# Back-to-back making of a head's two bf16 maxima parts on VectorE, in an attention and expert kernel on one Trainium2 core

## The chip, the cores and the metric

The kernel runs on one core of one Trainium2 chip. The metric is the device time of one execution in microseconds; the median of three runs of the kernel before is 1437.19 us (1435.57 to 1438.66). Engines are named as in the profile: PE is TensorE, PEld its weight loads, DVE is VectorE, ACT is ScalarE, POOL is GpSimd and SP is the engine that issues the DMAs.

## What is computed

A layer with gated attention and a gated mixture of experts. The attention, cut to what matters here:

```python
att = jnp.einsum('bhqd,bhkd->bhqk', q, k) * scale          # 4 batches, 16 heads, 512 queries, 512 keys, D=16
att = jnp.where(causal[None, None], att, -jnp.inf)
y = jnp.einsum('bhqk,bhkd->bhqd', jax.nn.softmax(att, axis=-1), v)
attc = jnp.einsum('bhqd,bhkd->bhqk', qc, kc) * scale       # the same queries on 1601 context rows
y = y + jnp.einsum('bhqk,bhkd->bhqd', jax.nn.softmax(attc, axis=-1), vc)
...
x = x + jnp.tanh(g_xattn[0]) * (y @ Wp + bp)
x = x + jnp.tanh(g_ffn[0]) * ffn(layernorm(x))             # a shared expert and 2 of 7 routed ones
```

Both softmaxes subtract a row's maximum, so each of the 64 (batch, head) pairs, called heads below, needs the maxima of its 512 queries over its own and over the cross scores before its exponentials are made.

## The kernel before

The program is written by hand: every engine has its own instruction stream and waits on counting semaphores, and there is no scheduler. It has three stages: preparation (projections, split into three bf16 parts, to about 153 us), the 64 heads (to about 936 us), and the projection, router and experts.

**One head.** A head's scores are computed twice on PE. The first time is for the maxima: 16 pieces (`MAX_PIECES`: 12 blocks of 128 queries by 512 context rows, one tail, three of the causal scores), each a product into a PSUM bank (`max_product`, mostly L525) and a reduction of it on DVE (`reduce_bank`, L1214). The second time the scores are made with keys on the partitions (`score`, L625 and L628), in 8 groups (`GROUPS`); two more rows of the stacked operands, made of the negated maxima, subtract each query's maximum in the product itself. ACT takes the exponential of each group (L967), and PE multiplies it with the values in 4 phases (`values`, L643).

**The maxima's way to the scores.** `max_parts(v, i)` on DVE makes them for head v in three instructions:

- i=0, L1226: the maximum over the five columns of `mx`, into `mneg[:, 1, :]`; signals `m_all`
- i=1, L1229: the negated maxima rounded to bf16, the high part, into `mparts[:, 0]`; waits for `m_all`, signals `m_hi`
- i=2, L1232: the rest, the low part, into `mparts[:, 1]`; waits for `m_hi`, signals `m_split`

Then `max_rows` on PE (L565 and L566) waits for `m_split` and turns them into rows by a product with the identity, ACT copies these to `rowst` (`rows`, L927), SP sends them to the stacked operand (`rows_load`, L448), and the next head's first score waits for the landing (`rows_ready`).

**The order on PE** is `schedule()`: in the step of head u it goes through groups g = 0 to 7; each brings the maxima's products 2g and 2g+1 around its scores. Product c of the step belongs to head u+1 (its pieces 8 to 15) for c below `HALF` = 8, and to head u+2 (its pieces 0 to 7) from c = 8 on. So the last piece of head u+1 is c = 7. The transposing product ("rows") comes after c = 11 and in front of the second value block (`values` 1). After product 7 come value block 0, the product that normalizes the head before ("norm", L692), and product 8.

**The banks.** Products c, "norm" and "rows" take three PSUM banks in turn (`ENTRIES`, `RING` = 3). `bank_free` therefore makes "rows" wait until DVE has reduced product 9, by the semaphore `max_red`, and only then does `max_rows` wait for `m_split`. Product 11 waits for the reduction of product 8 in the same way.

**The loop.** `run_steps` writes out heads 0 and 1, then a loop of 15 turns with four heads in its body, then heads 62 and 63. Inside the loop the values waited for lie in registers, so the engines' streams hold register additions.

Of the kernel before, what the change touches and what calls it, by code (L numbers as in the profile page):

```python
# [91 lines left out]
HALF = NMAX // 2  # L92
# [58 lines left out]
def program(nc, a):  # L151
    ctx = ExitStack()
    with ctx:
# [1020 lines left out]
        def _(dve):  # L1174
# [41 lines left out]
            def reduce_piece(u, c):  # L1216
                dve.wait_ge(S["max_mm"], u * NMAX + (c + 1))
                v, piece = (u + 1, c + HALF) if c < HALF else (u + 2, c - HALF)
                reduce_bank(v, piece, bank_of("max", c)).then_inc(S["max_red"], 1)

            def max_parts(v, i):

                if i == 0:
                    if not (isinstance(v, int) and v == 0):
                        dve.wait_ge(S["max_red"], v * NMAX + (NMAX - MAXED))
                    dve.tensor_reduce(mneg[:, 1, :], mx[:, :, :], AX_X, ALU.max).then_inc(S["m_all"], 1)  # L1226
                if i == 1:
                    dve.wait_ge(S["m_all"], v + 1)
                    dve.tensor_scalar(mparts[:, 0, :, :], mneg[:, :, :], -1.0, None, ALU.mult).then_inc(S["m_hi"], 1)  # L1229
                if i == 2:  # L1230
                    dve.wait_ge(S["m_hi"], v + 1)
                    dve.scalar_tensor_tensor(out=mparts[:, 1, :, :], in0=mneg[:, :, :], scalar=-1.0,  # L1232
                                             in1=mparts[:, 0, :, :], op0=ALU.mult, op1=ALU.subtract
                                             ).then_inc(S["m_split"], 1)
# [4 lines left out]
            for n, p in enumerate(pieces):  # L1239
# [24 lines left out]
                if p[0] == "max":  # L1264
                    _, v, c = p
# [25 lines left out]
            def reciprocals(u):  # L1291

                dve.wait_ge(S["sums_in"], u)
                if not (isinstance(u, int) and u == 1):
                    dve.wait_ge(S["y_parts"], u - 1)
                dve.reciprocal(rsum[:, :, :], sums[:, :, 2:4, D]).then_inc(S["rsum_ready"], 1)

            def step(u, r, prev, nxt, nxt2):
                for c in range(NMAX):
                    if (c < HALF and nxt) or (c >= HALF and nxt2):  # L1300
                        reduce_piece(u, c)
                    if nxt and HALF - 1 <= c < HALF + 2:
                        max_parts(u + 1, c - HALF + 1)
                    if prev and c == RSUM_AT:
                        reciprocals(u)

            run_steps(dve, step)
            reciprocals(NU)

# [276 lines left out]
```

## Time and profile before

| | us |
|---|---|
| median of 3 runs | 1437.19 |
| the profiled execution, its own time | 1437.22 |
| its span in the trace | 1435.5 |
| PE busy in the span | 1378.3 (96%) |
| DVE busy | 868.1 (60%) |
| ACT busy | 727.9 (51%) |
| POOL busy | 365.7 (25%) |

The busy time of PE holds modelled ends, and consecutive matmuls overlap in the records: two products of 512 columns stand some 0.22 us apart and are 0.38 us long each. So a short stop of PE shows less by its idle time than by the distance between starts. The same holds for DVE, where a reduction of 0.69 us is followed by the next instruction's start after 0.61 us.

### The profile page before, as it was taken

The page shows a single profiled execution, that of the slowest core. Times are in us where ns is not written, and L with a number is a line of the kernel's source. Part 1 is how long each engine was busy: PE and PEld are TensorE (multiplying, and loading weights), DVE is VectorE, ACT ScalarE, POOL GpSimd, SP SyncE. Part 2 cuts the span into 40 slices and gives each one's busy share as a digit, 9 for nine tenths or more (in the row PEclk, how much of TensorE's full clock was granted, in tenths as well). Part 3 has the DMA queues.
Part 4 walks back from the last instruction along what each step waited for, and adds up shares of the span by engine and source line. Part 5 has one row for each costly group of instructions (what it writes and reads, how often), then busy time and mean ns, then how long its engine had stood idle before and what let it go on. Part 6 is the DMA issues. An engine that isn't in the chain of part 4 may idle for free.

```text
span 1435.5 us, 27237 instructions
## 1 busy us (share of the span) xinstructions
PE 1378.3 (96%) x7688; PEld 697.9 (49%) x7689; DVE 868.1 (60%) x1804; ACT 727.9 (51%) x1107; POOL 365.7 (25%) x743
## 2 busy tenths in 40 slices
PE   7889899999999999999999999989999999999997
PEld 4445333333333333333333333354556677777775
DVE  6658688888888888888888888734532222222221
ACT  4534567767666767667676767652100222222221
POOL 5455322222222222222222222210000223323232
PEclk9989999999999999999999999999999999999999
DMA  7654211111111111111111111039003111212211
GB/s 240 206 159 146 85 52 51 49 49 48 48 46 49 50 51 50 49 49 47 47 48 48 50 51 50 18 143 364 0 1 117 40 30 29 37 29 31 34 29 23
DMA packets 57711, 98.43 MB, mean 69 GB/s; under 512 B 7441, under 2 KB 42001, under 8 KB 56657
## 3 DMA queue, kind: packets, MB, share of 16 engines
q1 hardware_dynamic: 50384, 88.10, 18.5%
q0 software_dynamic: 7296, 9.97, 4.3%
q8 instruction: 15, 0.25, 0.1%
q14 instruction: 16, 0.12, 0.0%
HBM read 69.20 MB, written 28.58 MB: 68 GB/s over the span
## 4 chain that ended last, share of the span: by engine, by line
PE 80%; issue 5%; DVE 4%; ACT 1%; DVEq 0%; DMA 0%; POOL 0%; POOLq 0%; SPq 0%; ACTq 0%
PE ps L643 18%; PE ps L808 13%; PE ps L625 10%; PE ps L525 10%; PE ps L821 7%; PE ps L760 5%; PE ps L771 3%; PE ps L692 3%; PE ps L539 2%; PE ps L832 2%; PE ps L628 2%; DVE mx L1214 1%; PE ps L529 1%; PE ps L566 1%; PE ps L599 1%
## 5 line engine op out<-in xcount | busy, mean ns | idle before, releaser
L1214 DVE TENSOR_REDUCE mx<-ps 128x1 f32<-128x512 f32 (+1 forms) x832 | 521.3, 663 | 127.0 <-PE ps L525 96.7
L967 ACT ACTIVATE arena<-ps 128x1024 f32<-128x1024 f32 (+1 forms) x512 | 484.5, 995 | 152.4 <-PE ps L625 148.7
L643 PE MATMUL ps<-arena 128*32 128x512 f32 (+5 forms) x2432 | 290.1, 524 | 0.6 <-ACT arena L967 0.4
L625 PE MATMUL ps<-arena 98*128 98x512 bf16 x832 | 264.2, 380 | 4.5 <-DMA arena<-rowst 4.5
L525 PE MATMUL ps<-arena 96*128 96x512 bf16 x768 | 263.4, 382 | 4.3 <-DVE arena L1279 2.4
L808 PE MATMUL ps<-arena,work 128*128 x608 | 186.4, 460 | 0.6 <-issue 0.6
L1116 POOL TENSOR_SCALAR_AFFINE_SELECT arena<-arena 128x128 f32<-128x128 f32 x256 | 74.8, 292 | 437.4 <-ACT arena L967 427.5
L525 PEld LDWEIGHTS ps<-arena 96*128 96x128 bf16 x768 | 74.3, 97 | 174.0 <-DVE mx L1214 103.2
L1489 DVE TENSOR_TENSOR work<-work,ps 128x352 f32<-128x352 f32 x76 | 39.6, 521 | 179.1 <-ACT work L1033 179.1
L808 PEld LDWEIGHTS ps<-arena,work 128*128 128x128 f32 x608 | 112.6, 190 | 57.4 <-issue 1.1
L1214 DVE TENSOR_REDUCE mneg<-ps 128x2 f32<-128x512 f32 (+2 forms) x192 | 112.4, 640 | 23.0 <-PE ps L535 23.0
L1033 ACT ACTIVATE work<-ps 128x352 f32<-128x352 f32 x76 | 35.2, 463 | 164.6 <-PE ps L808 164.6
L1158 POOL DMA_INDIRECT out<-bv,slot_table x38 | 59.8, 1575 | 207.3 <-DVE bv L1495 197.5
L643 PEld LDWEIGHTS ps<-arena 128*32 128x32 f32 (+1 forms) x2432 | 56.7, 108 | 113.5 <-issue 110.2
L625 PEld LDWEIGHTS ps<-arena 98*128 98x128 bf16 x832 | 76.7, 98 | 65.5 <-DMA arena<-rowst 5.7
L821 PE MATMUL ps<-arena,work 128*128 (+1 forms) x456 | 105.0, 379 | 0.8 <-ACT work L1039 0.8
L821 PEld LDWEIGHTS ps<-arena,work 128*128 128x128 f32 (+1 forms) x456 | 83.7, 190 | 11.4 <-issue 1.1
L1148 POOL DMA_INDIRECT wp<-xn_rows,slot_table x38 | 37.7, 992 | 173.4 <-DVE slot_table L1478 137.6
L1038 ACT ACTIVATE work<-ps 128x256 f32<-128x256 f32 x76 | 29.1, 382 | 99.7 <-PE ps L832 99.6
L760 PE MATMUL ps<-xnT,arena 128*128 128x512 f32 x176 | 77.1, 594 | 0.4 <-DVE work L1321 0.4
L1076 POOL TENSOR_TENSOR work<-arena,work 128x400 bf16<-128x400 f32 (+2 forms) x56 | 58.1, 1037 | 68.2 <-ACT work L919 67.4
L911 ACT ACTIVATE work<-ps,bqk 128x400 bf16<-128x400 f32 (+2 forms) x56 | 35.4, 632 | 64.7 <-DMA k_parts<-work 37.4
(157 smaller groups left out, 1411.0 us busy)
## 6 DMA issues: line engine op xcount, KB each, us to landing
arena<-in_experts SPq DMA_DIRECT2D x8, 2176.0 KB, 11.8
arena<-k_parts SPq DMA_DIRECT2D x64, 198.1 KB
arena<-k_parts SPq DMA_DIRECT2D x64, 132.1 KB
k_parts<-work SPq DMA_DIRECT2D x24, 300.0 KB, 4.2
q_parts<-work SPq DMA_DIRECT2D x16, 384.0 KB, 3.5
arena<-q_parts SPq DMA_DIRECT2D x64, 96.0 KB
arena<-k_parts SPq DMA_DIRECT2D x64, 66.0 KB
arena<-q_parts SPq DMA_DIRECT2D x64, 64.0 KB
```

Source lines behind the costliest of these rows:

```text
L525: mm = pe.matmul(out, qx[:, qt * P:(qt + 1) * P], ks[0:KROWS, T + j * CHUNK:T + (j + 1) * CHUNK], start=True, stop=True)
L625: mm = pe.matmul(bk[:, 0:w], kst[r][0:KROWS + MROWS, T + kt * P:T + (kt + 1) * P], qst[r][0:KROWS + MROWS, 1, :], start=True, stop=True)
L643: mm = pe.matmul(ps[32 * q:32 * q + VW, 6, b0:b1], vst[0:kn, r % VR, TT + kt if cross else kt, :], pr[0:kn, c0:c0 + b1 - b0], start=(phase ...
L692: mm = pe.transpose(out[:, t * P:(t + 1) * P], osb[:, t * P:(t + 1) * P], ident[:, :])
L760: mm = pe.matmul(ps[:, 2 * (k0 % 2) + j, :], wgus[:, k, w0:w0 + P], xnT[:, k, tb * T:(tb + 1) * T], start=(k == 0), stop=(k == 1))
L808: mm = pe.matmul(ps[:, 2 * c + j, 0:CH], xgT[:, b, k, :], weights[:, bass.ds(e, 1), o:o + CH], start=(k == 0), stop=(k == 1))
L821: mm = pe.matmul(ps[:, 4, 0:C], hidT[0:m, it, :], weights[0:m, bass.ds(e, 1), o:o + C], start=(it == 0), stop=(it == IT - 1))
L967: act.activation(pr[:, c0:c0 + n], ps[:, 2 * (g % 2):2 * (g % 2) + 2, :].rearrange("p b n -> p (b n)")[:, 0:n], ACT.Exp, scale=SCALE).then ...
L1076: pool.tensor_tensor(cut[:, s % NB, place_of(t)[2], 0:w], res[:, s % NB, 0:w], cut[:, s % NB, place_of(t)[1], 0:w], ALU.subtract).then_inc ...
L1116: pool.affine_select(out=exps, in_=exps, pattern=[[1, P]], compare_op=ALU.is_ge, fill=0.0, base=0, channel_multiplier=-1).then_inc(S["mask ...
L1158: pool.indirect_dma_start(out=a["out"], out_offset=bass.IndirectOffsetOnAxis(slot_table[:, i, 1:2], 0), in_=yt[:, i % 2, :], in_offset=Non ...
L1214: return dve.tensor_reduce(m, out, AX_X, ALU.max)
```

## The change

In the step of head u, DVE made the three instructions of `max_parts(u + 1, ...)` with a reduction between each two of them: reduction 7, part 0, reduction 8, part 1, reduction 9, part 2, reduction 10. They now stand behind reduction 7 together, in front of reduction 8. PE's order does not change, nor do those of ACT, POOL and SP.

```diff
                 for c in range(NMAX):
                     if (c < HALF and nxt) or (c >= HALF and nxt2):
                         reduce_piece(u, c)
-                    if nxt and HALF - 1 <= c < HALF + 2:
-                        max_parts(u + 1, c - HALF + 1)
+                    if nxt and c == HALF - 1:
+                        for i in range(3):
+                            max_parts(u + 1, i)
                     if prev and c == RSUM_AT:
                         reciprocals(u)
```

VectorE in a head of the loop, before. `mneg<-ps` are the reductions of products 6 and 7 (causal pieces), `mx<-ps` those of products 8, 9 and on; REGISTER_ALU and ISA are instructions of the engine's sequencer that compute a semaphore's value, and two of them carry a wait.

```order
L1214 TENSOR_REDUCE mneg<-ps 128x1 [waits max_mm]
L1225 ISA
L1226 TENSOR_REDUCE mneg<-mx 128x4 [waits max_red]
L1217 REGISTER_ALU
L1203 REGISTER_ALU [waits max_mm]
L1214 TENSOR_REDUCE mx<-ps 128x1 [waits m_all]
L1229 TENSOR_SCALAR mparts<-mneg 128x8 [waits m_all]
L1217 REGISTER_ALU
L1214 TENSOR_REDUCE mx<-ps 128x1 [waits max_mm]
L1232 SCALAR_TENSOR_TENSOR mparts<-mneg,mparts 128x8 [waits m_hi]
L1217 REGISTER_ALU
L1214 TENSOR_REDUCE mx<-ps7 128x1 [waits max_mm]
```

The same place of the same head in the changed kernel:

```order
L1214 TENSOR_REDUCE mneg<-ps 128x1 [waits max_mm]
L1225 ISA
L1226 TENSOR_REDUCE mneg<-mx 128x4 [waits max_red]
L1228 REGISTER_ALU
L1229 TENSOR_SCALAR mparts<-mneg 128x8 [waits m_all]
L1232 SCALAR_TENSOR_TENSOR mparts<-mneg,mparts 128x8 [waits m_hi]
L1217 REGISTER_ALU
L1214 TENSOR_REDUCE mx<-ps 128x1 [waits m_all,max_mm]
L1217 REGISTER_ALU
L1214 TENSOR_REDUCE mx<-ps 128x1 [waits max_mm]
L1217 REGISTER_ALU
L1214 TENSOR_REDUCE mx<-ps7 128x1 [waits max_mm]
```

Both parts moved ahead of the reductions of products 8 and 9, and the register instruction of L1203, which waited for product 8, is gone: the reduction carries both waits itself.

TensorE around the transposing product (L566), which is the same in both kernels; L625 and L628 are scores, L525 the maxima's products 9, 10 and 11:

```order
L525 MATMUL ps<-arena 128x512 [waits max_red]
L525 MATMUL ps7<-arena 128x512 [waits norm_evac]
L656 REGISTER_ALU
L625 MATMUL ps<-arena 128x512 [waits exp_done]
L628 MATMUL ps<-arena 128x256
L628 MATMUL ps<-arena 128x128
L551 REGISTER_ALU
L525 MATMUL ps<-arena 128x512 [waits max_red]
L551 REGISTER_ALU
L566 MATMUL ps<-identb,mparts 16x128 [waits m_split,max_red]
L636 REGISTER_ALU [waits exp_done]
L643 MATMUL ps<-arena 32x512 [waits masked]
```

Nothing moves here: L566 keeps its two waits, for the bank (`max_red`) and for the parts (`m_split`).

## Rows read from the trace of the kernel before

**Rows 1.** The page's first line.
```profile
span 1435.5 us, 27237 instructions
```
**Rows 2.** Busy time by stretch, the heads: us, engines, granted clock, DMA.
```profile
162.00:936.00 774.00, 763.18 (x5229) 292.50 (x5226) 624.69 (x1240) 542.19 (x687) 182.80 (x560) 1.00 0.15 47
```
**Rows 3.** Line 566, the transposing product: durations; what ended idle time before.
```profile
L566 PE MATMUL ps<-identb,mparts x64: 216/218/223, 132.4 to 932.6; 128*16 128x128 bf16 x64
...
  DVE mparts L1232: 29.2, 86
```
**Rows 4.** Timeline of DVE, a head of the loop: start us, us, instruction.
```profile
707.40 0.17 DVE L1226 TENSOR_REDUCE mneg<-mx 128x4 f32<-128x16 f32 x1
708.38 0.69 DVE L1214 TENSOR_REDUCE mx<-ps 128x1 f32<-128x512 f32 x1 [0.81 <-PE ps L525]
708.99 0.16 DVE L1229 TENSOR_SCALAR mparts<-mneg 128x8 bf16<-128x8 f32 x1
709.06 0.68 DVE L1214 TENSOR_REDUCE mx<-ps 128x1 f32<-128x512 f32 x1
709.66 0.16 DVE L1232 SCALAR_TENSOR_TENSOR mparts<-mneg,mparts 128x8 bf16<-128x8 f32 x1
```
**Rows 5.** Timeline of PE, the same head: products 8, 9 with 10, 11, transpose.
```profile
707.87 0.38 PE L525 MATMUL ps<-arena 96*128 96x512 bf16 x1
...
708.53 0.59 PE L525 MATMUL ps<-arena 96*128 96x512 bf16 x2
...
709.34 0.38 PE L525 MATMUL ps<-arena 96*128 96x512 bf16 x1
709.87 0.22 PE L566 MATMUL ps<-identb,mparts 128*16 128x128 bf16 x1
```
**Rows 6.** The fourth head of the loop's body: DVE, then PE.
```profile
734.49 0.16 DVE L1232 SCALAR_TENSOR_TENSOR mparts<-mneg,mparts 128x8 bf16<-128x8 f32 x1
```
```profile
733.36 0.59 PE L525 MATMUL ps<-arena 96*128 96x512 bf16 x2
...
734.79 0.22 PE L566 MATMUL ps<-identb,mparts 128*16 128x128 bf16 x1 [0.24 <-DVE mparts L1232]
```
**Rows 7.** A head ahead of the loop: DVE, then PE.
```profile
161.01 0.69 DVE L1214 TENSOR_REDUCE mx<-ps 128x1 f32<-128x512 f32 x1 [0.39 <-PE ps L525]
...
162.29 0.16 DVE L1232 SCALAR_TENSOR_TENSOR mparts<-mneg,mparts 128x8 bf16<-128x8 f32 x1
```
```profile
160.58 0.39 PE L525 MATMUL ps<-arena 96*128 96x512 bf16 x1
...
162.59 0.22 PE L566 MATMUL ps<-identb,mparts 128*16 128x128 bf16 x1 [0.15 <-DVE mparts L1232]
```
**Rows 8.** Sequencer's instructions of lines 565 (PE) and 1203 (DVE), durations in ns.
```profile
L565 PEldq ALU_OP  x45: 32/32/32, 199.9 to 921.2; - x45
L565 PEldq EVENT_SEMAPHORE  x19: 51/51/51, 130.9 to 931.9; - x19
```
```profile
L1203 DVEq ALU_OP  x60: 40/40/40, 185.9 to 919.7; - x60
```
**Rows 9.** Timeline of DVE where the parts already stand together, the last head.
```profile
931.23 0.17 DVE L1226 TENSOR_REDUCE mneg<-mx 128x4 f32<-128x16 f32 x1
...
931.64 0.17 DVE L1232 SCALAR_TENSOR_TENSOR mparts<-mneg,mparts 128x8 bf16<-128x8 f32 x1
```
**Rows 10.** The same in the preparation: DVE, then POOL at that time.
```profile
130.15 0.67 DVE L1232 SCALAR_TENSOR_TENSOR mparts<-mneg,mparts 128x8 bf16<-128x8 f32 x1
```
```profile
130.07 0.73 POOL L1083 TENSOR_TENSOR x<-x,bv 128x256 f32<-128x256 f32 x1 [0.17 <-POOL work L1076]
```
**Rows 11.** Timeline of POOL in the head of rows 4.
```profile
707.26 0.29 POOL L1116 TENSOR_SCALAR_AFFINE_SELECT arena<-arena 128x128 f32<-128x128 f32 x1 [2.01 <-ACT arena L967]
708.62 0.31 POOL L1105 TENSOR_TENSOR router<-router 128x68 f32<-128x68 f32 x1 [1.06 <-ACT router L956]
```
**Rows 12.** Timeline of ACT behind that transpose; who waited for line 448's DMA.
```profile
711.91 1.94 ACT L967 ACTIVATE arena<-ps 128x1024 f32<-128x1024 f32 x2 [1.22 <-PE ps L625]
```
```profile
  PE ps L625: 4.5, 2
```

## The prediction

> **What bounds the kernel now.** I start with the busy time by stretch. Over the 774 us of the heads PE is busy for 763 us at full granted clock (1.00), DVE for 625 and ACT for 542 [rows 2]. So PE sets the pace, and DVE and ACT matter only where PE stops for them. ACT confirms it: behind the transposing product's group its next exponentials find it idle for 1.22 us, waiting for PE's scores [rows 12].
>
> PE's idle time can't show short stops, since its records overlap. So the second view is the timeline of one head, read by the distance between starts. Products 9 and 10 start at 708.53 and take 0.59 us as a pair of overlapping records of 0.38 us, so products of 512 columns follow each other after 0.21 to 0.22 us. Product 11 starts at 709.34, and PE could start what follows at 709.56. The transposing product starts at 709.87 [rows 5]. PE stands still for 0.31 us there. What it waits for is in the view of its line: idle time before L566 was ended by L1232, DVE's low part, 86 times (PE and its weight loads counted apart) [rows 3]. In the timeline the low part ends at 709.66 + 0.16 = 709.82, and L566 follows 0.05 us later [rows 4, 5].
>
> **What the change moves.** It adds and removes no arithmetic. Two instructions of 0.16 us each go from between the reductions to in front of reduction 8. Five questions follow.
>
> *1. Do the parts fit there?* DVE ends part 0 at 707.40 + 0.17 = 707.57 and is idle until reduction 8 at 708.38, which waits for product 8 [rows 4]. Where the three already stand together, the low part starts 0.41 us behind part 0 and ends 0.58 us behind it, waits on their own results included [rows 9]. From 707.40 that gives an end at 707.98. Even 0.1 us more for register instructions leaves 0.2 us before the new start of reduction 8 below. The cost is nothing; the cover is DVE's wait for product 8. Queued behind the new waits are reductions 8 to 10, and they are not delayed.
>
> *2. When does reduction 8 start?* In the loop it starts 708.38 - 707.87 = 0.51 us behind product 8 [rows 4, 5]. Ahead of the loop it starts 161.01 - 160.58 = 0.43 us behind it [rows 7]. The difference of 0.08 us is the wait that sits on a register instruction of L1203, which stands there in all 60 heads of the loop [rows 8]. The change takes that instruction out and the reduction carries the wait. I take 0.43: reduction 8 starts at 708.30.
>
> *3. When does reduction 9 end?* On DVE it could start 0.61 us after reduction 8 (the spacing of 708.38 and 708.99), at 708.91; product 9 allows 708.53 + 0.43 = 708.96. The later one holds, and with 0.68 us it ends at 709.64 instead of 709.74 [rows 4, 5].
>
> *4. When does PE go on?* The parts are ready long before, and L566's other wait, the bank that reduction 9 frees, now ends last. The price of that handover isn't shown, since today it comes first. The nearest rows bound it: 0.05 us where PE's last wait is on the instruction itself [rows 4, 5], and 0.14 to 0.15 us in the heads where another wait instruction comes in between (162.45 to 162.59) [rows 7]. There is more than one form: in 45 heads the bank's wait sits on a register instruction (ALU_OP), in 19 an EVENT_SEMAPHORE stands in front of L566 [rows 8]. For the 45 I take 0.05 plus the 0.08 that such a register instruction costs DVE in question 2: 0.13 us. L566 starts at 709.64 + 0.13 = 709.77, against 709.87. The gain is **0.10 us in each of 45 heads**.
>
> For the fourth head of the loop's body (15 of the 19) L566 starts 734.79 - 734.65 = 0.14 us behind the low part, 0.09 more than in the others [rows 6]. I read this as the EVENT_SEMAPHORE taking the `m_split` wait and L566 itself the bank's. Then the late wait changes from the slow form to the direct one. Reduction 9 ends at 733.36 + 0.43 + 0.69 = 734.48, and 0.05 us later is 734.53. The gain is **0.26 us in each of 15 heads**. If the slow form stays, it is 0.16.
>
> The transposes in the steps of heads 0 and 1 have DVE's direct form already, so reduction 9 gains almost nothing; they gain the 0.08 us that the low part ends behind reduction 9 (709.82 against 709.74) and 0.09 of handover (0.14 against 0.05): 0.17 us each. The transposes of head 0's own maxima and of the last head are unchanged, since the parts stand together there now.
>
> *5. What is late next?* Value block 1, behind L566, and everything on PE after it move ahead by the gain. ACT's copy of the turned rows follows its own exponentials and does not move, and the DMA behind it doesn't either. Only two score products in the whole trace waited for that DMA, 4.5 us in sum [rows 12], so the loop's heads have room. The later exponentials, masks and reductions wait for PE and move with it. Nothing gives the gain back.
>
> **The sum.** 45 x 0.10 + 15 x 0.26 + 2 x 0.17 = 4.5 + 3.9 + 0.3 = 8.7 us. The profiled execution took 1437.22 us (span 1435.5 [rows 1]), and the median of the runs is 1437.19, so both lead to **1428.5 us**, 0.6% faster. With 0.15 us of handover everywhere the gains are 0.08, 0.16 and 0.08: 3.6 + 2.4 + 0.2 = 6.2 us, 1431.0. With 0.05 everywhere they are 0.18, 0.26 and 0.17: 8.1 + 3.9 + 0.3 = 12.3 us, 1424.9.
>
> One rule speaks against question 3. The rows show that DVE starts the next instruction before the last has ended: the high part starts at 708.99, reduction 8 ends at 709.07 [rows 4]. The Trainium skill (VectorE: DVE Perf Modes, "The DRAIN you can't avoid") says the next instruction does not start until the pipeline has emptied. By it reduction 9 would start at 708.30 + 0.69 = 708.99 and the 45 heads would gain 0.07 instead of 0.10, 1.4 us less in all. The trace does not agree, so the sum stands.
>
> **The rivals.**
>
> *A. Only the slot is gained (1432.2 to 1432.9).* Reduction 8 keeps its 0.51 us, because its two waits cost as much as the register instruction did, and PE's handover stays at today's forms. Then reduction 9 ends 0.07 us earlier, PE's wait moves from the low part's end, 0.08 after reduction 9's, to reduction 9's own, and a handover dearer by 0.08 takes that back: about 0.07 to 0.08 us x 62 = 4.3 to 5.0 us. For it: the double wait on reduction 8 is of a form that the loop doesn't show. Against it: [rows 7] shows that same pair of waits at 0.43. Chance 0.14.
>
> *B. A wait takes the stop's place (about 1437).* If the bank's handover costs 0.05 + 0.17 us or more in most heads, or a later product was held by something that does not move (an exponential, a mask, the stacked operands' DMA), the shift ends there. Against it: ACT idles for 1.22 us after the transpose [rows 12], and the head's pace is PE's [rows 2]. Chance 0.06.
>
> *C. The low part gets long, and it is slower (about 1441).* In the preparation the same instruction took 0.67 instead of 0.17 us, and it ended with a POOL operation of two inputs that ran from 130.07 to 130.80 [rows 10]. In the new place everything on DVE queues behind it. At that length the low part would end at 707.40 + 0.41 + 0.67 = 708.48, reduction 8 would start there or up to 0.08 before it, and each L566 would come up to 0.06 us later than now: 708.48 + 0.61 + 0.68 + 0.13 = 709.90, plus register instructions. That is some 0.03 to 0.1 us x 62, 2 to 6 us. It decides from a start of reduction 8 at about 708.45. Against it: POOL's selection ends at 707.55, its next operation starts at 708.62 [rows 11], and the low part would run from 707.81 to 707.98, with nothing beside it. Chance 0.04. The Trainium skill (VectorE: DVE Perf Modes, "Two Vector instructions with no wait between them") names a read interface for second inputs that is shared with GpSimd; the long row agrees with it.
>
> *D. The whole stop goes (about 1417).* All 0.31 us in 45 heads and more in 15, some 20 us. It would need L566 not to wait for reduction 9. The bank's ring excludes that: 709.64 is later than 709.56. Chance 0.01.
>
> **How the numbers follow.** The forecast's case has 0.75 and runs from 1424.9 to 1431.0, its likeliest value is 1428.5. The range takes in rival A and leaves the rare ends out: 1425.2 to 1433.0. A measurement of this kernel tells about 0.2%, 2.9 us, from no change. The forecast, A and D are faster by more than that, less a little of A's edge: 0.89. B and a small remainder are within it: 0.08. C is slower by more: 0.03.
>
> **What the changed profile would show.** High and low part stand 0.2 us apart behind part 0, each 0.16 to 0.17 us, with DVE idle after them (question 1, rival C). Reduction 8 starts 0.43 us behind product 8 (question 2; 0.51 is rival A). Reduction 9 directly follows, 0.65 us later. L566 starts 0.43 us behind product 11 in three heads of four and 0.35 in the fourth, instead of 0.53 and 0.62, and its releaser is L1214 instead of L1232. From the transpose at 709.87 to the one at 734.79, two heads with a fourth one, it is 24.92 us now; it becomes 24.56 (0.10 and 0.26 less). If the starts are right but the period isn't, question 5 is wrong. The forecast fails if the bank's handover costs over 0.2 us.

## The result and the profile after

| | before | after |
|---|---|---|
| median us | 1436.42 (4 runs) | 1428.72 (4 runs, 1428.34 to 1429.37) |
| ratio | | 0.9944, 95% interval 0.9927 to 0.9962 |
| profiled span us | 1435.5 | 1427.5 |
| one body of the loop, four heads, us | 49.75 | 49.13 |

The change makes the kernel 0.56% faster; the forecast was 1428.5 us. The last row is worked out from the starts of the transposing product: from one place of the loop's body to the same place 14 turns later, divided by 14. The loop runs 15 times, so its heads gave 15 x 0.62 = 9.3 us, in that profile. The two transposes ahead of the loop gave 0.35 us more. The span fell by 8.0 us, so the rest of the program took some 1.7 us more in that profile; how far it varies is shown by the last experiment (e9).

What is called the fourth head of the loop's body, in [rows 6] and below, comes first in the body by time: its transposes are those of heads 3, 7 and so on to 59, and the first lies in the step of head 2, with which the loop begins. The sums don't depend on the name.

The page after, its first line and busy PE (the counterparts of [rows 1] and of the table before):

```profile
span 1427.5 us, 27297 instructions
...
PE 1376.8 (96%) x7688; PEld 698.2 (49%) x7689; DVE 882.3 (62%) x1804; ACT 728.6 (51%) x1107; POOL 367.2 (26%) x743
```

DVE's busy time rises by 14 us while the time falls. Records that used to overlap their neighbours (the small parts between two reductions) now stand in a gap and are counted in full. That is no cost.

Timeline of DVE in an ordinary head after (start us, us, instruction), beside [rows 4]:

```profile
713.23 0.17 DVE L1226 TENSOR_REDUCE mneg<-mx 128x4 f32<-128x16 f32 x1
713.44 0.17 DVE L1229 TENSOR_SCALAR mparts<-mneg 128x8 bf16<-128x8 f32 x1
713.64 0.17 DVE L1232 SCALAR_TENSOR_TENSOR mparts<-mneg,mparts 128x8 bf16<-128x8 f32 x1
714.12 0.69 DVE L1214 TENSOR_REDUCE mx<-ps 128x1 f32<-128x512 f32 x1 [0.32 <-PE ps L525]
...
714.77 0.69 DVE L1214 TENSOR_REDUCE mx<-ps 128x1 f32<-128x512 f32 x1
```

Timeline of PE in the same head, beside [rows 5]: products 8, 9 with 10, 11, and the transposing product.

```profile
713.71 0.38 PE L525 MATMUL ps<-arena 96*128 96x512 bf16 x1
...
714.36 0.60 PE L525 MATMUL ps<-arena 96*128 96x512 bf16 x2
...
715.17 0.38 PE L525 MATMUL ps<-arena 96*128 96x512 bf16 x1
715.60 0.22 PE L566 MATMUL ps<-identb,mparts 128*16 128x128 bf16 x1
```

The same rows in the fourth head of the loop's body, beside [rows 6]:

```profile
727.48 0.38 PE L525 MATMUL ps<-arena 96*128 96x512 bf16 x1
727.83 0.22 PE L566 MATMUL ps<-identb,mparts 128*16 128x128 bf16 x1
```

The low part ends at 713.81, and DVE waits 0.32 us more for product 8. Reduction 8 starts 0.42 us behind that product (713.71; 0.51 before). Reduction 9 ends at 715.46, and L566 follows at 715.60, 0.13 us later, 0.42 us behind product 11 instead of 0.53 (medians over the loop, here and below; single rows can differ by 0.01). In the fourth head it is 0.35 instead of 0.62.

Line 566's waits, beside [rows 3], and line 1203's, beside [rows 8]:

```profile
  issue: 17.0, 46
  DVE mx L1214: 5.5, 18
```

```profile
L1203 DVEq EVENT_SEMAPHORE  x63: 21/21/21, 131.3 to 910.3; - x63
```

L1232 ends no wait any more. Where a register instruction lies between reduction 9's signal and the product, the view says "issue" (46 times). The 60 register additions of line 1203 that waited for product 8 are gone; in their place a wait for part 0, which has long been met, stands ahead of the reduction.

### The profile page after: what moved, and what is told of

It reads as the page before. It is cut to its first block, busy times and chain, and to the rows that moved or that the text cites. A ratio compares the mean times of both kernels' runs of the same rounds, so it can differ in the third digit from the quotient of the medians.

```text
span 1427.5 us, 27297 instructions
## 1 busy us (share of the span) xinstructions
PE 1376.8 (96%) x7688; PEld 698.2 (49%) x7689; DVE 882.3 (62%) x1804; ACT 728.6 (51%) x1107; POOL 367.2 (26%) x743
## 4 chain that ended last, share of the span: by engine, by line
PE 87%; DVE 2%; ACT 1%; issue 1%; DMA 0%; POOL 0%; POOLq 0%; SPq 0%; ACTq 0%; DVEq 0%
PE ps L643 18%; PE ps L808 13%; PE ps L625 13%; PE ps L525 12%; PE ps L821 7%; PE ps L760 5%; PE ps L771 3%; PE ps L692 3%; PE ps L628 2%; PE ps L832 2%; PE ps L539 2%; PE ps L529 1%; PE ps L566 1%; PE ps L599 1%; PE ps L514 1%
## 5 line engine op out<-in xcount | busy, mean ns | idle before, releaser
L1214 DVE TENSOR_REDUCE mx<-ps 128x1 f32<-128x512 f32 (+1 forms) x832 | 515.1, 662 | 98.5 <-PE ps L525 68.2
L625 PE MATMUL ps<-arena 98*128 98x512 bf16 x832 | 264.1, 380 | 4.7 <-DMA arena<-rowst 4.7
L525 PE MATMUL ps<-arena 96*128 96x512 bf16 x768 | 263.3, 382 | 4.7 <-DVE arena L1279 2.8
L525 PEld LDWEIGHTS ps<-arena 96*128 96x128 bf16 x768 | 74.3, 97 | 174.5 <-DVE mx L1214 103.9
L625 PEld LDWEIGHTS ps<-arena 98*128 98x128 bf16 x832 | 76.6, 98 | 65.7 <-DMA arena<-rowst 5.9
L821 PEld LDWEIGHTS ps<-arena,work 128*128 128x128 f32 (+1 forms) x456 | 83.6, 190 | 11.4 <-issue 1.1
```

Of the source, the lines that this page charges most:

```text
L525: mm = pe.matmul(out, qx[:, qt * P:(qt + 1) * P], ks[0:KROWS, T + j * CHUNK:T + (j + 1) * CHUNK], start=True, stop=True)
L625: mm = pe.matmul(bk[:, 0:w], kst[r][0:KROWS + MROWS, T + kt * P:T + (kt + 1) * P], qst[r][0:KROWS + MROWS, 1, :], start=True, stop=True)
L821: mm = pe.matmul(ps[:, 4, 0:C], hidT[0:m, it, :], weights[0:m, bass.ds(e, 1), o:o + C], start=(it == 0), stop=(it == IT - 1))
L1214: return dve.tensor_reduce(m, out, AX_X, ALU.max)
```

## The experiments

Besides medians each is read by the time of the loop's body, worked out as above. It leaves out preparation and experts, so it tells hundredths of a microsecond apart. The third column is worked out from unrounded bodies.

| kernel | body of four heads, us | x 15 against before, us | median against the kernel before in its group, us |
|---|---|---|---|
| before | 49.75 | | |
| after | 49.13 | -9.3 | 1428.72, -7.7 |
| e1, low part behind reduction 9 | 49.32 | -6.5 | 1429.98, -6.4 |
| e5, register wait gone, parts old | 49.41 | -5.2 | 1428.09, -6.9 |
| e2, transpose behind value block 1 | 48.51 | -18.7 | 1416.22, -20.1 |
| e3, the same with the parts old | 48.51 | -18.7 | 1417.10, -19.3 |
| e4, PE's waits swapped | 48.83 | -13.9 | 1422.33, -14.0 |
| e10, the same with the parts old | 49.95 | +3.1 | 1436.79, +2.1 |
| e6, parts behind reduction 8 | 50.54 | +11.9 | 1447.23, +12.2 |
| e7, low part twice | 49.13 | -9.3 | 1424.09, -10.9 |
| e8, low part four times | 50.16 | +6.1 | 1441.36, +6.4 |
| e11, POOL beside the low part | 50.30 | +8.3 | 1443.82, +9.1 |
| e9, after again | 49.13 | -9.3 | 1424.98, -9.7 |

### Which part of the change pays: e1 and e5

The low part alone goes back:

```diff
                     if nxt and c == HALF - 1:
-                        for i in range(3):
+                        for i in range(2):
                             max_parts(u + 1, i)
+                    if nxt and c == HALF + 1:
+                        max_parts(u + 1, 2)
```

> The changed kernel with one part undone: parts 0 and 1 stay behind reduction 7, the low part goes back behind reduction 9. The computation is whole. My theory (three terms: the register instruction of L1203 gone, the low part off the path, the wait form in the fourth heads): reduction 8 still starts 0.43 us behind product 8, but the low part again ends 0.08 us behind reduction 9 and PE waits for it. In the 45 ordinary heads the two nearly cancel (0.08 for the low part and 0.05 for a direct wait, against 0.13 for the register form): L566 stays at 0.42 to 0.43 us behind product 11. In the 15 fourth heads it goes back from 0.35 to 0.52, 0.17 x 15 = 2.6 us: 1431.3 us. The rival, that the low part's place alone made the gain: all of it goes, L566 at 0.53 and 0.62, 1436 us. A second rival, that the order of the parts is of no matter and the gain came from elsewhere: 1428.7.

PE in an ordinary head starts L566 0.42 us behind product 11, as with the whole change. Below, the fourth head of that run: 0.51 us, against 0.35.

```profile
728.07 0.38 PE L525 MATMUL ps<-arena 96*128 96x512 bf16 x1
728.58 0.22 PE L566 MATMUL ps<-identb,mparts 128*16 128x128 bf16 x1
```

So moving the low part is worth nothing in 45 heads and 0.16 us in 15. In the 45 two things cancel: the low part, moved back, ends 0.07 us behind reduction 9, but L566 follows its end after 0.06 us, where it follows reduction 9's after 0.13. By the body of the loop it is 0.18 x 15 = 2.8 us where 2.6 was expected. The median, 1429.98, stands 1.3 us above the changed kernel's in another group of runs; the loop's body is the surer measure.

The other side: nothing is moved, only the order of reduction 8's two waits in the kernel before.

```diff
             def reduce_piece(u, c):
-                dve.wait_ge(S["max_mm"], u * NMAX + (c + 1))
                 v, piece = (u + 1, c + HALF) if c < HALF else (u + 2, c - HALF)
+                if piece == 0:
+                    dve.wait_ge(S["m_all"], v)
+                dve.wait_ge(S["max_mm"], u * NMAX + (c + 1))
```

> The kernel before, its parts still between the reductions. Only the order of reduction 8's two waits is changed: the wait for part 0 (m_all) comes first, and now sits on the register instruction, the wait for product 8 sits on the reduction itself. The computation is whole. My theory (term of question 2): reduction 8 starts 0.42 us behind product 8 in all heads instead of 0.505 in the loop, everything on DVE up to the low part comes 0.085 us earlier, L566 at 0.446 and 0.533 us behind product 11 instead of 0.531 and 0.62, and 0.085 x 60 = 5.1 us go: 1431.3 us, without any part moved. The rival, that this distance is of the product and not of the wait's form: 1436.4 us.

DVE in an ordinary head of that run, the parts still between the reductions; product 8 started at 702.47:

```profile
702.89 0.69 DVE L1214 TENSOR_REDUCE mx<-ps 128x1 f32<-128x512 f32 x1 [0.72 <-PE ps L525]
703.50 0.16 DVE L1231 TENSOR_SCALAR mparts<-mneg 128x8 bf16<-128x8 f32 x1
703.57 0.69 DVE L1214 TENSOR_REDUCE mx<-ps 128x1 f32<-128x512 f32 x1
704.17 0.16 DVE L1234 SCALAR_TENSOR_TENSOR mparts<-mneg,mparts 128x8 bf16<-128x8 f32 x1
```

Reduction 8 starts 0.42 us behind its product, and L566 0.445 and 0.53 us behind product 11 (0.53 and 0.62 before), both as expected. More than half of what the change gives (5.2 of 9.3 us) is this register instruction, and none of that comes from taking small instructions from between the reductions. It vanished as a side effect: the high part needs the same value of `m_all`, and where it stands ahead of reduction 8 the value has been computed (L1228 in the changed order). The runs agree: in e1, with only the low part back, L1203 carries no register instruction, and in e6 below, with both parts behind reduction 8, it has its 60 again.

The last piece is the high part. With it between the reductions (e5) reduction 9 starts 0.44 us behind product 9, without it (e1) 0.42, and e1's bodies are 0.09 us shorter: 1.3 us. So the gain in the loop is 5.2 us for the register wait, 1.3 for the high part and 2.8 for the low part.

### What is left of the stop, and whether the place of the parts matters without it: e2 and e3

```diff
         if g == 5:
-            out += [("rows",), ("values", 1)]
+            out += [("values", 1), ("rows",)]
```

> The changed kernel, and on PE the transposing product stands behind value block 1 instead of in front of it. The computation is whole. My theory: what is left of PE's stop (0.21 us in 45 heads, 0.13 in 15, 0.15 in 2) is the wait for reduction 9, and value block 1, some 1 us of work, covers it: L643 starts 0.22 us behind product 11, L566 shows no wait, and 0.21 x 45 + 0.13 x 15 + 0.15 x 2 = 11.7 us go: 1417.0 us. The rows' DMA is issued about 1.76 us behind product 11 and lands 1.8 us later, 0.8 us ahead of the next head's first score. The rival: the maxima's rows come too late (ACT's copy or the DMA), the next head's first score waits, and the time is 1428 us or more.

> The kernel before, with its parts between the reductions, and on PE the transposing product behind value block 1. The computation is whole. My theory: the change under study pays only through PE's stop in front of L566. Without that stop the place of the parts is of no matter: the same time as with the parts back to back and the transposing product behind value block 1, 1417.0 us, within 1.5 us. The rival, that parts between reductions cost DVE or a later product something of their own: 3 us or more above that run.

PE behind product 11, from e2:

```profile
719.70 0.38 PE L525 MATMUL ps<-arena 96*128 96x512 bf16 x1
720.01 1.06 PE L643 MATMUL ps<-arena 128*32 128x512 f32 x8
720.89 0.22 PE L566 MATMUL ps<-identb,mparts 128*16 128x128 bf16 x1
721.05 0.39 PE L525 MATMUL ps<-arena 96*128 96x512 bf16 x1
```

The stop is gone: the value block starts 0.31 us behind product 11, and L566 follows without a wait. The body of the loop is the same to a hundredth in both, with the parts back to back or between the reductions. So the change under study pays only through PE's stop in front of L566, and with the transpose in the other place it gives nothing. The rows' DMA came in time. The stop was worth 9.4 us by the loop's bodies (0.63 x 15), where 11.4 of the expected 11.7 lay in the loop. I had put the value block 0.22 us behind product 11, and it starts 0.31 behind it. Part of that comes back: in the new place the transpose lengthens the way from the value block's start to the next product from 0.99 to 1.03 us (720.01 to 721.05), by 0.04, where in the old place it took 0.11 us in front of the block.

**e2 beats both kernels**: 1416.22 us, ratio to the kernel before 0.9858 (0.9843 to 0.9873).

### The price of PE's handover: e4 and e10

In front of the transposing product the wait for the parts is written ahead of the wait for the bank, first in the changed kernel, then in the one before.

```diff
                     elif item[0] == "rows" and nxt:
+                        pe.wait_ge(S["m_split"], u + 2)
                         bank_free(u, "rows")
```

> The changed kernel; on PE, in front of the transposing product, the wait for the parts (m_split) stands before the wait for the bank (max_red), so that the wait that ends last sits on the product itself and not on a register instruction in front of it. The computation is whole. My theory: the handover from reduction 9's end to L566 falls from 0.13 to 0.05 us in the 45 ordinary heads, L566 starts 0.35 us behind product 11 in all heads of the loop, and 0.077 x 45 = 3.5 us go: 1425.2 us. The rival, that the handover takes 0.13 us whatever the form and the fourth heads differ for another reason: 1428.7 us.

> The kernel before, its parts between the reductions; on PE the wait for the parts (m_split) stands before the wait for the bank (max_red). The computation is whole. The same edit made the changed kernel faster by 0.076 us per ordinary head. My theory: a wait is cheap when it sits on the waiting product and comes last. Here the parts' wait comes last and moves onto the register instruction: L566 comes 0.13 us behind the low part's end instead of 0.05, at 0.61 us behind product 11 in all heads of the loop, 0.53 before in 45 and 0.62 in 15: 0.077 x 45 - 0.015 x 15 = 3.2 us slower than the kernel before. The rival, that this order of the waits is better whatever comes last: 3 to 5 us faster than the kernel before.

PE in an ordinary head of e4, then of e10:

```profile
711.27 0.38 PE L525 MATMUL ps<-arena 96*128 96x512 bf16 x1
711.62 0.22 PE L567 MATMUL ps<-identb,mparts 128*16 128x128 bf16 x1
```

```profile
721.29 0.38 PE L525 MATMUL ps<-arena 96*128 96x512 bf16 x1
721.89 0.22 PE L567 MATMUL ps<-identb,mparts 128*16 128x128 bf16 x1 [0.23 <-DVE mparts L1234]
```

In e4 L566 (here L567) starts 0.35 us behind product 11 in every head of the loop, 0.05 us behind reduction 9's end. In e10 it starts 0.60 us behind product 11 in every head. One edit, both signs: the wait that ends last is cheap on the waiting instruction (0.05 us) and dear on a register instruction in front of it (0.13). e4 gained 4.6 us by the loop's bodies (0.31 x 15) where 3.5 was expected. The rest is the value block behind it: it starts 0.09 us behind L566 instead of 0.11, in the fourth heads of the changed kernel already. Why, the rows don't tell. Beside e1, e4 also shows what moving the low part can give: 0.08 us in every head (0.35 against 0.42 behind product 11), which the changed kernel pays back to the register form in 45 of them.

### How deep the cover is: e7, e8 and e6

The low part is made twice, or four times, each waiting for the one before (shown for twice):

```diff
-                    dve.wait_ge(S["m_hi"], v + 1)
-                    dve.scalar_tensor_tensor(out=mparts[:, 1, :, :], in0=mneg[:, :, :], scalar=-1.0,
-                                             in1=mparts[:, 0, :, :], op0=ALU.mult, op1=ALU.subtract
-                                             ).then_inc(S["m_split"], 1)
+                    steps = ["m_hi", "m_low0", "m_split"]
+                    for waited, done in zip(steps, steps[1:]):
+                        dve.wait_ge(S[waited], v + 1)
+                        dve.scalar_tensor_tensor(out=mparts[:, 1, :, :], in0=mneg[:, :, :], scalar=-1.0,
+                                                 in1=mparts[:, 0, :, :], op0=ALU.mult, op1=ALU.subtract
+                                                 ).then_inc(S[done], 1)
```

> The changed kernel with the low part made twice in a row, each waiting for the one before it (the same values again). The computation is whole. It measures how deep the cover is. My theory: the chain of parts ends 0.79 us behind part 0's start, reduction 8 can't start before 0.89 (ordinary) or 0.80 us (fourth heads) because of product 8, so nothing moves: 1428.7 us, L566 at 0.424 and 0.348 us behind product 11. The rival, that DVE's time in front of reduction 8 is on the path: + 0.206 x 60 = 12.4 us, 1441.1 us.

> The changed kernel with the low part made four times in a row, each waiting for the one before it (the same values again). The computation is whole. My theory: now the cover is gone. The chain ends 1.20 us behind part 0's start and reduction 8 starts at 1.10 to 1.13 us instead of 0.89 and 0.80, reduction 9 follows it after 0.61 us, so L566 comes 0.17 to 0.20 us later in ordinary and 0.26 to 0.29 in fourth heads: 45 x 0.18 + 15 x 0.27 = 12.2 us, 1440.9 us. The rival, that 0.6 us more of small instructions on DVE still hide: 1428.7 us.

Twice costs nothing: the body of the loop is the changed kernel's. DVE with four, where the cover ends:

```profile
710.30 0.17 DVE L1226 TENSOR_REDUCE mneg<-mx 128x4 f32<-128x16 f32 x1
710.51 0.17 DVE L1229 TENSOR_SCALAR mparts<-mneg 128x8 bf16<-128x8 f32 x1
710.71 0.77 DVE L1234 SCALAR_TENSOR_TENSOR mparts<-mneg,mparts 128x8 bf16<-128x8 f32 x4
711.48 0.69 DVE L1214 TENSOR_REDUCE mx<-ps 128x1 f32<-128x512 f32 x1
```

Reduction 8 starts 1.18 us behind part 0 instead of 0.89, without idle time in front of it. Seen from product 8, L566 comes 0.23 us later in ordinary heads and 0.32 in fourth ones, where 0.18 and 0.27 were expected. I had let reduction 8 start ahead of the last low part's end, as it does behind a reduction; here it starts only with that end. In the fourth heads 0.07 of the 0.32 us is product 11, which waits for reduction 8 and starts 0.89 us behind product 9 instead of 0.82.

The cover taken away, one place further back:

```diff
                     if nxt and c == HALF - 1:
-                        for i in range(3):
+                        max_parts(u + 1, 0)
+                    if nxt and c == HALF:
+                        for i in (1, 2):
                             max_parts(u + 1, i)
```

> The changed kernel with the pair of bf16 parts moved one place back: part 0 behind reduction 7, the high and the low part back to back behind reduction 8, in front of reduction 9. The computation is whole. It takes the cover away: at this place DVE isn't waiting. My theory: DVE pays the chain in full, reduction 9 starts 0.61 + 0.21 + 0.07 = 0.89 us behind reduction 8 instead of 0.65, reduction 8 is back at 0.505 us, reduction 9 ends 0.61 us behind product 11, and L566 stands at 0.74 us in ordinary heads and 0.66 in fourth ones. Against the changed kernel 0.317 x 45 + 0.315 x 15 = 19.0 us, 1447.7 us, which is 11 us slower than the kernel before. The rival, that back to back is what pays, wherever it stands: 1429 to 1432 us.

```profile
716.81 0.69 DVE L1214 TENSOR_REDUCE mx<-ps 128x1 f32<-128x512 f32 x1 [0.81 <-PE ps L525]
717.42 0.16 DVE L1229 TENSOR_SCALAR mparts<-mneg 128x8 bf16<-128x8 f32 x1
717.62 0.18 DVE L1232 SCALAR_TENSOR_TENSOR mparts<-mneg,mparts 128x8 bf16<-128x8 f32 x1
717.72 1.28 DVE L1214 TENSOR_REDUCE mx<-ps 128x1 f32<-128x512 f32 x2
```

Reduction 9 starts 0.91 us behind reduction 8. Ordinary heads came out as expected (0.76 against 0.74 us behind product 11), the fourth ones did not: 0.75 instead of 0.66, since there reduction 9 started 0.98 us behind reduction 8. Those 0.07 us are in the low part. In the fourth heads it takes 0.25 us instead of 0.18 and ends 0.02 us behind a sum on POOL that began ahead of it (DVE, then POOL):

```profile
742.90 0.25 DVE L1232 SCALAR_TENSOR_TENSOR mparts<-mneg,mparts 128x8 bf16<-128x8 f32 x1
```

```profile
742.80 0.33 POOL L1107 TENSOR_TENSOR router<-router 128x68 f32<-128x68 f32 x1
```

So this is rival C's mechanism, which the next experiment tests, and it shows here with one of the kernel's own POOL operations. The median, 1447.23, is 12.2 us slower than the kernel before. Back to back pays only in a gap.

### The mechanism that would have made it slower: e11

```diff
                 mask(u, 1, 2)
+                if nxt:
+                    pool.tensor_tensor(beside[:, 2, :], beside[:, 0, :], beside[:, 1, :], ALU.add).then_inc(S["beside"], 1)
+                    pool.wait_ge(S["beside"], u + 1)
```

`beside` is 3 x 384 columns of a region that nothing else uses during the heads.

> The changed kernel, and POOL adds two unused stretches of 384 columns (about 1.1 us) behind its second causal selection in every head but the last, so that it runs beside the high and the low part's new place. What the kernel computes is whole; the sum is read by nobody. It measures rival C of the prediction. If DVE's two-input instruction is held while POOL reads two inputs, as in the preparation, the low part starts 0.41 us behind part 0 and ends with POOL's sum, about 1.3 us behind part 0, reduction 8 starts at 1.2 us instead of 0.89 and 0.80, and L566 comes 0.29 us (ordinary) and 0.38 us (fourth) later: 45 x 0.29 + 15 x 0.38 = 18.8 us more than the changed kernel, 1443 to 1448 us. The rival, that the long low part of the preparation had another cause: the low part stays at 0.17 us and the time within 1 us of the changed kernel in this group of runs.

DVE, then POOL, in an ordinary head:

```profile
710.88 0.17 DVE L1233 TENSOR_SCALAR mparts<-mneg 128x8 bf16<-128x8 f32 x1
711.09 0.85 DVE L1236 SCALAR_TENSOR_TENSOR mparts<-mneg,mparts 128x8 bf16<-128x8 f32 x1
```

```profile
710.92 1.00 POOL L1130 TENSOR_TENSOR arena<-arena 128x384 f32<-128x384 f32 x1
```

The low part takes 0.85 us (median of all 64: 845 ns) and ends at 711.94, with POOL's sum at 711.92. The high part keeps its 0.17 us, but it started 0.03 us ahead of the sum. In the fourth heads the sum starts first (DVE, then POOL):

```profile
736.03 0.97 DVE L1233 TENSOR_SCALAR mparts<-mneg 128x8 bf16<-128x8 f32 x1
737.03 0.17 DVE L1236 SCALAR_TENSOR_TENSOR mparts<-mneg,mparts 128x8 bf16<-128x8 f32 x1
```

```profile
735.97 1.00 POOL L1130 TENSOR_TENSOR arena<-arena 128x384 f32<-128x384 f32 x1
```

There the high part, with its single input, is the one that is held: 0.97 us in all 15, with its end 0.03 us behind the sum's, and the low part behind it takes 0.17. So a second input is not the condition. In every head of the loop the part held is the one that starts first while the sum runs; other instructions and other operations beside them were not tried.

Against the changed kernel the loop's bodies take 1.17 x 15 = 17.6 us more (18.8 expected). The sum came near by two misses of opposite sign. Seen from product 8, L566 comes 0.22 us later in ordinary heads (0.29 expected) and 0.52 in fourth ones (0.38 expected), since there the low part comes behind the held high part, and product 11, which waits for reduction 8, starts 1.08 us behind product 9 instead of 0.82.

The Trainium skill (VectorE: DVE Perf Modes, "Two Vector instructions with no wait between them") names a read interface shared with GpSimd, for the second of two SBUF inputs and for the single input of an instruction in a 2-port mode. The low part's rows agree with the first; whether the high part runs in such a mode no row shows.

In the changed kernel itself both parts keep 0.17 us in every head of the loop. The margin is small. POOL's last operation ahead of them ends at 713.38, and the high part starts at 713.44:

```profile
713.09 0.29 POOL L1116 TENSOR_SCALAR_AFFINE_SELECT arena<-arena 128x128 f32<-128x128 f32 x1 [2.02 <-ACT arena L967]
```

### How much lies outside the heads: e9

> The changed kernel once more, unaltered, to see how far the time outside the heads differs from one profile to the next. The run with the low part made twice has the changed kernel's period in the heads to the nanosecond (12.282 us) and yet a median 4.6 us lower, in another group of runs. If that is the spread of what lies outside the heads, this one comes out anywhere from 1424 to 1429 us with a period of 12.28 us, and its preparation and last stage differ from the first profile's by 1 to 3 us. The rival, that making the low part twice is faster for a reason of its own: 1428.7 again, with the first profile's preparation and last stage.

The changed kernel once more gave 1424.98 us, 9.7 below the kernel before of its group (1434.71), ratio 0.9930 (0.9917 to 0.9944), with the same body of the loop. Its first transpose in the preparation came at 130.3 us instead of 132.9, and its span was 1424.4 instead of 1427.5 us. So making the low part twice is not faster for itself, and medians of different groups differ by some 4 us for one and the same kernel. What in the preparation differs was not settled. The loop's bodies do not vary: they agree to a hundredth of a microsecond.

## Why the prediction was right, point by point

**The number.** 1428.5 was forecast and 1428.72 measured; that they agree to 0.2 us is luck. The heads gave 9.6 us where the sum has 8.7, the rest of the program took some 1.7 us more in that profile, and the same kernel gave 1424.98 us in another group (e9). What the runs bear out is the mechanism, term by term.

**What bounds.** PE, with one stop in front of L566. Right: e2 takes the stop away and 18.7 us go, and e3 shows that the parts' place is then of no matter.

**1, the parts fit.** Right. They end 0.58 us behind part 0's start (713.81 against 713.23), as in [rows 9]. One more instruction of 0.2 us still fits (e7), three more don't (e8).

**2, reduction 8 starts 0.43 us behind product 8.** Measured 0.42. Right for the reason given: e5 gets the same with the parts unmoved. The text treated it as a side term; it is the larger part of the gain.

**3, reduction 9 ends 0.10 us earlier.** Right: held by product 9, it starts 0.65 us behind reduction 8, by the emptying rule it would have been 0.69. In e8 and e11, where nothing else holds it, it starts 0.60 to 0.61 us behind one of 0.69 us. The Trainium skill (VectorE: DVE Perf Modes, "The DRAIN you can't avoid") states the emptying rule and adds that a next instruction that is not held starts earlier. For two reductions the trace agrees with the addition, which the prediction left out, and not with the rule. Small instructions chained by their own results stand fully apart (0.20 to 0.21 us at 0.17).

**4, the handover.** 0.13 us in ordinary heads and 0.05 in the fourth ones, both as put, and e4 and e10 show that the wait's form is the cause. The gains per head were 0.107 and 0.272 us at L566 where the text had 0.10 and 0.26. In the fourth head the value block also follows 0.02 us sooner, which the sum had not. That makes 9.3 us in the loop instead of 8.4. The two transposes ahead of the loop gained 0.16 and 0.18 us, where 0.17 each was put.

**5, nothing gives it back.** Right: from the transpose at 703.29 to the one at 727.83, two heads with a fourth one, it is 24.54 us, where the forecast was 24.56 and the kernel before had 24.92. The loop's body fell by 0.62; the gains at L566 add up to 3 x 0.107 + 0.272 = 0.59, and the value block's 0.02 is most of the rest.

**The rivals.** A falls with e5 and e4, which show both forms' prices. B falls with the period. C's mechanism is real (e11, and e6); it didn't happen because POOL stands idle there. C looked only at the low part: the high part, which starts 0.2 us earlier and some 0.05 us behind POOL's selection, can be held as well. D falls because 0.13 to 0.21 us of the stop remain, counted from the 0.22 us that stand between two products; its time was reached only by changing PE's order (e2).

## What to carry to other kernels

When two waits stand in front of one instruction, write the one that ends last directly before it, after any value that must be computed for the other; here that was worth 0.08 us per wait in a loop, on PE (e4) and on VectorE (e5) alike, and the wrong way round cost 0.07 us in 45 heads (e10). Small instructions are free only inside a gap whose end another engine sets: read the gap's length and who ends it before moving them, and what POOL does at that time. And before polishing what a stopped engine waits for, look whether other work of that engine can go in front of the wait: that was worth twice as much (e2).

## What was not expected of the hardware

- A VectorE instruction of 8 columns that started while POOL made a sum was held until that sum's end, whether it had two SBUF inputs (0.17 to 0.85 us) or one (0.17 to 0.97 us), and ended 0.02 to 0.03 us behind it. One that had started 0.03 us ahead of the sum kept its 0.17 us. In the profile this is a long instruction and not a wait.
- A reduction behind another reduction of 0.69 us starts after 0.60 to 0.61 us, ahead of its end; behind a chain of 0.17 us instructions it started only at their end (711.48 in e8).
- Four heads written with the same statements in a loop's body don't get the same wait instructions: three had a register addition carrying PE's wait for the bank, the fourth an EVENT_SEMAPHORE carrying its wait for the parts, and that made 0.09 us of difference before the change.
